# Layer 3 of a four-layer graph kernel: adjacency rows loaded in two streams, and one product moved ahead of another on VectorE

## What is computed

```python
def _logmap(x, y, c):
    sub = _mobius_add(-x, y, c)
    sub_norm = jnp.maximum(jnp.linalg.norm(sub, axis=-1, keepdims=True), MIN_NORM)
    lam_x = 2.0 / jnp.maximum(1.0 - c * x2, MIN_NORM)
    arg = jnp.clip(sqrt_c * sub_norm, 0.0, TANH_CLIP)
    return 2.0 / (sqrt_c * lam_x) * jnp.arctanh(arg) * sub / sub_norm

w = adj / deg
log_ij = _logmap(x[:, None, :], x[None, :, :], c)
agg = jnp.einsum('ij,ijc->ic', w, log_ij)
```

## Time and profile before

| | us |
|---|---|
| median of 3 runs | 1580.62 |
| lowest and highest run | 1574.34, 1580.66 |
| the profiled execution: its time | 1574.34 |
| the profiled execution: its span | 1572.6 |
| layer 3's units, first product to last sum | 1112.6 to 1515.3 |

### The profile page before, as it was taken

The page is one execution under the profiler, slowest core; times in us unless marked ns, Lnnn a source line. Parts: engine busy times, 40 slices in busy tenths (PEclk is TensorE's granted clock), DMA queues, the critical chain, the costliest instruction groups (busy, mean ns, idle before and its releaser), DMA issues. The chain is left out here.

```text
span 1572.6 us, 20194 instructions
## 1 busy us (share of the span) xinstructions
PE 1410.9 (90%) x7727; PEld 613.7 (39%) x7752; DVE 1231.7 (78%) x1631; ACT 927.0 (59%) x880; POOL 230.0 (15%) x149
## 2 busy tenths in 40 slices
PE   5999999789977699999999999979989999999970
PEld 1433333223324344444454454534434444444440
DVE  4899866676776877967978967547798888999877
ACT  0000286358643545445445546767788889989964
POOL 1000000000000000000000000243254444444430
PEclk9999999999998799999999999999999999999995
DMA  9999699979999255544534431233635464555600
GB/s 338 409 409 409 246 405 410 413 286 399 410 414 412 92 184 195 180 164 167 182 134 179 182 123 46 89 120 123 214 121 173 149 196 153 178 170 158 203 15 27
DMA packets 135896, 348.93 MB, mean 222 GB/s; under 512 B 7732, under 2 KB 57208, under 8 KB 135544
## 3 DMA queue, kind: packets, MB, share of 16 engines
q1 hardware_dynamic: 119968, 329.27, 56.7%
q10 hardware_dynamic: 15832, 18.36, 3.3%
HBM read 329.78 MB, written 17.83 MB: 221 GB/s over the span
## 5 line engine op out<-in xcount | busy, mean ns | idle before, releaser
L988 PE MATMUL ps<-ring,X 128*64 128x512 f32 x512 | 264.2, 598 | 15.2 <-DVE ring L2149 15.1
L989 PE MATMUL ps<-work,X 128*64 128x512 f32 x512 | 264.3, 598 | 0.0
L1479 ACT ACTIVATE work<-ring 128x2048 f32<-128x2048 f32 x64 | 122.3, 1911 | 157.1 <-PE ps L996 123.6
L994 PE MATMUL ps<-work 128*64 128x512 bf16 x768 | 208.5, 380 | 0.0
L996 PE MATMUL ps<-work 128*64 128x512 bf16 x768 | 208.5, 380 | 0.0
L755 POOL TENSOR_TENSOR ring<-ring,work 128x1024 f32<-128x1024 f32 x72 | 171.0, 2375 | 235.3 <-DVE work L2412 235.2
L857 PE MATMUL ps<-ring,work 128*64 128x512 f32 x672 | 158.1, 615 | 22.5 <-DMA ring<-in_adjT 22.5
L718 POOL TENSOR_SCALAR work<-ring 128x1024 int16<-128x1024 uint8 x24 | 28.2, 1179 | 1010.7 <-DMA ring<-codes 938.3
L994 PEld LDWEIGHTS ps<-work 128*64 128x64 bf16 x768 | 84.9, 111 | 177.9 <-issue 152.5
L1105 PE MATMUL ps<-work 128*128 128x512 f32 x288 | 145.7, 629 | 0.0
L1305 ACT ACTIVATE work<-work,code_bias 128x2048 uint8<-128x2048 bf16 (+1 forms) x32 | 62.3, 1947 | 91.9 <-DVE work L1892 79.0
(11 more groups left out here) (365 smaller groups left out, 2790.3 us busy)
## 6 DMA issues: line engine op xcount, KB each, us to landing
ring<-in_adjT SPq DMA_DIRECT2D x88, 2048.0 KB, 16.4
work<-in_adjT SPq DMA_DIRECT2D x28, 2048.0 KB, 20.7
ring<-in_adjT SPq DMA_DIRECT2D x24, 1024.0 KB, 9.5
ring<-in_adjT SPq DMA_DIRECT2D x48, 512.0 KB, 3.7
ring<-codes SPq DMA_DIRECT2D x32, 512.0 KB, 3.7
ring<-in_adjT SPq DMA_DIRECT2D x64, 256.0 KB, 3.1
codes<-work ACTq DMA_DIRECT2D x32, 256.0 KB, 6.2
codes<-work ACTq DMA_DIRECT2D x64, 128.0 KB, 1.7
```

The lines of the kernel that those rows point to most:

```text
L988: nc.tensor.matmul(ps[0:F, h, :], rows, ring[:, r, k, cols], start=start, stop=stop)
L989: nc.tensor.matmul(ps[F:P, h, :], rows, negs[:, pair, i, cols], start=start, stop=stop)
L994: nc.tensor.matmul(ps[0:F, 2 + h, :], part, more[:, pair, i, cols], start=start and t == 0, stop=stop and t == 2)
L1479: nc.scalar.activation(negs[:, pair], ring[:, s % RING, 2 * pair:2 * pair + 2, :], ACT.Relu, scale=-1.0).then_inc(negs_made, 1)
```

## The change

Two things change.

First, the edge rows of layer 3. The one ring of six becomes two: O units use four tile rows (`ring[:, 0]`), which are loaded two units at a time by one DMA of 1 MB (`load_off`, every second O unit), and I and D units use two tile rows (`ring[:, 1, 0:2]`, `load_own`). A pair of O rows is loaded once the O unit three before the pair's first has been gathered; an I or D row once the I or D unit two before has been gathered. The strips are as before. SP sorts the loads by the unit that they wait for.

Second, in VectorE's loop `multiply(units[n + 1])` is called before `mirror_weights(units[n - 2], 1)`. The calls of PE, ACT and POOL stand in the order in which they stood.

```diff
--- before.py
+++ after.py
@@ -214,8 +214,6 @@
 
 
 
-        edge_rows = [ring[:, i, k, :] for i, k in ((0, 0), (0, 1), (1, 0), (1, 1), (0, 2), (0, 3))]
-        EDGE_ROWS = len(edge_rows)
         SETS = ((0, 1, 4, 5), (2, 3, 6, 7))
         TURN_OF = SETS[0] + SETS[1]
         ORDERS = ["OOODOODODOODIIOODOOD", "OOOODIDIOOODODOOOO", "OOOODIDIOOOOOOOO", "OOOODIDIOOOOOOOODD"]
@@ -274,9 +272,7 @@
                     done = ends.index(u) + 1
         for u in units:
             u.sums = 4 if u.off else 5
-            u.row = u.n % EDGE_ROWS
-            u.edges = edge_rows[u.row]
-            u.arrived = (units[u.n - EDGE_ROWS].arrived if u.n >= EDGE_ROWS else 0) + (16 if u.off else 32)
+            u.edges = ring[:, 0, u.place % 4, :] if u.off else ring[:, 1, u.place % 2, :]
         quad_opens, quad_ends, quad_turns = [], [], []
         for u in units:
             if not u.turned:
@@ -458,7 +454,7 @@
         mirror_weighted = sem("mirror_weighted")
         mirrored = sem("mirrored")
         direct_added = sem("direct_added")
-        edges_in = [sem(f"edges_in{r}") for r in range(EDGE_ROWS)]
+        edges_in = [[sem(f"edges_in{i}_{r}") for r in range(2)] for i in range(2)]
         strip_in = [sem(f"strip_in{r}") for r in range(2)]
         mirror_added = sem("mirror_added")
         moved_made = sem("moved_made")
@@ -617,16 +613,20 @@
                 src = codes_dram[Q * NS + s:Q * NS + s + 1].rearrange("a h p n -> p (a h) n")
                 sp.dma_start(code_in[:, r].rearrange("p h k c -> p h (k c)"), src).then_inc(code_loaded[r], 16)
 
-            def load_edges(u):
-
-                if u.off:
-                    b = u.rows[0]
-                    sp.dma_start(u.edges, adj_slots[:, b // GB, b % GB, u.I, :]).then_inc(edges_in[u.row], 16)
-                    return
+            def load_off(u):
+
+                r = u.place // 2 % 2
+                b = u.rows[0]
+                src = adj_slots[:, b // GB:b // GB + 1, b % GB:b % GB + 2, u.I:u.I + 1, :].rearrange(
+                    "p a k b c -> p (a k) (b c)")
+                sp.dma_start(ring[:, 0, 2 * r:2 * r + 2], src).then_inc(edges_in[0][r], 16)
+
+            def load_own(u):
+
                 for h, b in enumerate(u.rows):
                     src = u.columns(adj_slots[:, b // GB, b % GB, u.I, :], h)
                     sp.dma_start(u.edges[:, h * HALF:(h + 1) * HALF].rearrange("p (t c) -> p t c", t=2), src).then_inc(
-                        edges_in[u.row], 16)
+                        edges_in[1][u.place % 2], 16)
 
             def load_strip(quad):
 
@@ -646,21 +646,23 @@
                 sp.wait_ge(pair_used, 2 + 2 * (SLOTS - RING + r + 1))
                 load_strip(r - 2)
             wait_for_codes_read(SLOTS - 2)
-            for u in units[0:2]:
-                load_edges(u)
+            load_off(off_units[0])
             sp.wait_ge(decay_used, SLOTS - 2)
-            for u in units[2:4]:
-                load_edges(u)
+            for u in own_units[0:2]:
+                load_own(u)
             wait_for_codes_read(SLOTS)
-            for u in units[4:EDGE_ROWS]:
-                load_edges(u)
-            turns = [(u.n - EDGE_ROWS + 1, 0, u.n) for u in units[EDGE_ROWS:]]
-            turns += [(quad_ends[q - 2] + 1, 1, q) for q in range(2, len(quad_ends))]
+            load_off(off_units[2])
+            turns = [(own_units[i - 2].n + 1, 0, i) for i in range(2, len(own_units))]
+            turns += [(off_units[i - 3].n + 1, 1, i) for i in range(4, len(off_units), 2)]
+            turns += [(quad_ends[q - 2] + 1, 2, q) for q in range(2, len(quad_ends))]
             for done, kind, i in sorted(turns):
                 if kind == 0:
                     sp.wait_ge(gathered, done)
-                    load_edges(units[i])
+                    load_own(own_units[i])
                 if kind == 1:
+                    sp.wait_ge(gathered, done)
+                    load_off(off_units[i])
+                if kind == 2:
                     sp.wait_ge(mirror_weighted, quad_turns[i - 2])
                     load_strip(i)
 
@@ -751,7 +753,10 @@
 
             for u in units:
                 pool.wait_ge(g_made, u.n + 1)
-                pool.wait_ge(edges_in[u.row], u.arrived)
+                if u.off:
+                    pool.wait_ge(edges_in[0][u.place // 2 % 2], (u.place // 4 + 1) * 16)
+                else:
+                    pool.wait_ge(edges_in[1][u.place % 2], (u.place // 2 + 1) * 32)
                 nc.gpsimd.tensor_tensor(u.edges, u.edges, u.angle, ALU.mult).then_inc(weighted, 1)
                 if u.n == 2:
                     pool.wait_ge(weighted, u.n + 1)
@@ -2420,10 +2425,10 @@
                                            u.angle, ALU.max, ALU.add).then_inc(sum_made, 1)
                 if n == 0:
                     copy_nodes(2)
+                if unit_at(n + 1):
+                    multiply(units[n + 1])
                 if turned_at(n - 2):
                     mirror_weights(units[n - 2], 1)
-                if unit_at(n + 1):
-                    multiply(units[n + 1])
                 if n == 0:
                     copy_sums2(NQ - 1)
                 if n == 2:
```

## The result

The changed kernel takes 1624.24 us (median of four runs, 1620.43 to 1636.71), against 1579.19 for the kernel before (four runs by now): ratio 1.0304, 95% interval 1.0244 to 1.0366. It is slower by 45 us, where +24 was forecast; 1624.24 lies just above the end of the range. The profiled execution took 1634.02, which is 10 above the median. In it the first product of layer 3 starts at 1121.6 us, 9.0 later than in the trace of the kernel before, though of what lies ahead of it only the first edge loads were changed; over all the traces here that start lies between 1112 and 1122.

The account below looks back on a forecast made before the run. PE, nearly full, and a dependency ring were taken to set the 5.35 us period. Terms 23.0 + 1.0 - 5.2 + 6.6 = +25.4 us on 1574.34 gave 1599.7, from the median 1606; 1603 was taken, range 1586 to 1624.

Parts of the forecast that it names:

- the two mechanisms: Layer 3: PE's transposes wait for the mirror product moved behind the product; edge rows land late behind strip and pair loads.
- the first periods: Layer 3's first 17 periods, seven with both units turned: each costs 0 to 0.72 us, 1 us taken for all.
- the stalls: Gathers of units 26, 44 and 60: rows land late behind a strip and 1 MB pair, 3 x 2.2 = +6.6 us.
- The ring through the transposes: Later periods with units n-2 and n-1 turned: 6.07 us instead of 5.35, 32 x 0.72 = 23.0 us.
- The two periods that I had left at 0: Two of 34 later turned periods: PE's move of points ahead of the second half's transposes covers the wait, 0 us.
- The gain near D units: 20 periods from 19 on with a D unit at n-1 or n-2: 0.26 us shorter each, -5.2 us.
- The clock rival: 52 later periods: PE idle 0.7 of 6.07 us, so its clock falls, 0.38 us each, +20, 1623; chance 9%.
- The rival of loads late in more places: Units 27, 45, 61 and some pairs: ten more places at 2 us on top, +45, 1623; chance 14%.

Follow-up runs that it names:

- the run meant to show it: Changed kernel with 24 transposes of the identity on PE ahead of the gathers of units 26, 44 and 60: 1621.21 us, ratio 1.0259.

## Why the prediction was too small

The direction and the two mechanisms were right; the size was not. Some 20 us are missing, and two terms of the sum, taken at 7.6 us together, hold 12 to 19 of them: the first periods at 1 us and the stalls at 6.6. The step that failed is that both were priced one by one and at the full clock, with the clock left to a rival that was not added. In its place the runs showed 8.4 us for the first and 11.5 to 18.1 for the second. By its own steps:

- **The ring through the transposes: right, under-sized by little.** Forecast 6.07 us, measured 6.13. The 0.06 between mirror product and transposes is 0.15 in this place. The two periods that I had left at 0 stayed there (7.17 us each, 7.27 before). The 33 periods cost 24.2 us, forecast 23.0, and with the fall of the clock that lies among them 25.8.
- **The gain near D units: right.** Forecast -5.2, measured -5.2 over 18 periods: 5.02 us in the mean, where I had 5.04 as ACT's limit.
- **The first periods: the term that failed by the largest factor.** I wrote that "the new ring is no longer than what is there, so each costs between 0 and 0.72, and I take 1 us for all". The order there alone costs 8.4 us by the medians. The period's length was the wrong thing to compare, since it leaves out the clock. At an equal 10.2 us at 1.2 GHz the order costs 2.6 us here in the one trace that shows it; the traces with 20.5 to 34.1 us at 1.2 GHz are 8 to 13 us over the kernel before. PE is the least busy in this part (84% in the first window before, 78% with the new order there). That the added waits bring the clock down more often is how the runs look; what decides in which execution it falls stays open.
- **The stalls: the place right, the size not.** The place, the strip and the pair ahead, POOL's wait and the landing (9.3 us forecast, 10.1 and with the loads alone 9.4 measured) are as forecast, and 6.6 us stands against 4.9 with the loads alone. The 1 MB load of a pair, which no run had shown, lands in 5.3 us (median) where a load of 512 KB took 3.7: 1.6 more, where I had added 2.0. What I left out is that the two edits work on each other: the new order issues the strip 1.4 us later against the row and shortens the periods before the use, so PE stands 2.8 to 3.9 us instead of 1.2 to 2.3, and behind such a wait its clock fell more often. Against the order alone the three periods cost 18.1 us in one trace and 11.5 in the other.
- **The clock rival** had 9% and the argument that 87% busy had kept a full clock. It was priced at +20 us, about what is missing, but spread over all turned periods, and there the clock falls only one to three times in a trace. Most of its time at 1.2 GHz lies in the first periods and behind the stalls: in the first trace of the changed kernel 51 us of layer 3 up to the last product, in the second 24, in the kernel before 10.
- **The rival of loads late in more places** (14%) did not come true: POOL waited for a DMA at units 13, 26, 44 and 60 alone. At unit 13, taken at 0, the gather waited 0.42 us.

The sum with the measured terms: 25.8 - 5.2 + 8.4 + 11.5 to 18.1 = 40.5 to 47.1, against +45. (The two traces of the changed kernel are of runs of 1634.02 and 1612.17 us, on either side of its median.) By the medians, without the table, it is 25.6 for the order and 18 to 20 for what hangs on the strips. The traces suggest that the clock falls because PE has stood, but the run meant to show it did not decide, and how much of the stalls' cost is the clock is not shown by a run.

## What to carry to other kernels

Before an instruction is moved ahead of another on one engine, look at who waits for the one that is now later, and what stands behind that waiter in its queue: 0.4 us gained on VectorE cost 0.8 us a period here, because PE's transposes stood ahead of the work that feeds ACT. Where only some periods have that waiter, the move can be kept for the others, and that made the fastest version. When two edits are priced, price them together once: a load asked for later and an order that releases the transfer ahead of it later add up to more than the two (45 us here, where each alone costs 25.6 and 4.3).

## What was not expected of the hardware

TensorE's clock did not fall in 43 us at 86% busy, with six waits of 0.75 us and one of 1.62. It did fall behind single waits, but not behind each. In the six traces with VectorE's new order and PE's transposes in their old place, from period 19 on, a fall came behind 2 of 175 waits of 0.3 to 1.0 us, behind 9 of 34 waits of about 1.6 us, and behind 6 of 8 waits of 2.8 to 3.9 us. Of the six gathers of the changed kernel's two traces it was four. With the loads alone, where the waits were 2.29, 1.20 and 2.04 us, it was one, the last. So a longer wait was followed by a fall more often, and how long it is does not tell by itself.

The time at 1.2 GHz differs between executions of one kernel and spreads the runs: 1.0% with the order in the first 19 periods alone, 0.6% for the kernel before beside it. A single trace can then mislead by 8 us in 19 periods, as the first one of the changed kernel did.
